# The attention's last product made transposed in three fp32r parts, and turned back through DRAM

## The reference

```python
    x = L0_attn_x
    x = x + _layernorm(_L0_attn_ref(_layernorm(x, axis=-1), L0_attn_gamma, L0_attn_beta, L0_attn_w_qkv, L0_attn_w_out, L0_attn_b_out), axis=-1)
    x = x + _layernorm(_L0_ffn_ref(_layernorm(x, axis=-1), L0_ffn_Wg, L0_ffn_Wu, L0_ffn_Wd), axis=-1)
    return x
```

```python
        qkv = jnp.einsum('bnc,ck->bnk', xn, w_qkv)
...
        k = jax.nn.softmax(k, axis=1)
        context = jnp.einsum('bnhd,bnhe->bhde', k, v)
        out = jnp.einsum('bhde,bnhd->bnhe', context, q)
        out = out.reshape(b, n, HEADS * DIM_HEAD)
        out = jnp.einsum('bnk,kc->bnc', out, w_out) + b_out
        return out + x
```

## Time and profile before

| what | value |
|---|---|
| median of the runs | 547.89 us |
| profiled execution, device time | 547.71 us |
| span of its trace | 545.9 us |
| PE busy | 538.5 us (99%) |
| DVE busy | 439.1 us (80%) |
| ACT busy | 344.5 us (63%) |
| POOL busy | 163.6 us (30%) |
| steady batch (100.00 to 165.43 us) | PE busy all the time at full granted clock |

### The profile page before, as it was taken

The page is one execution under the profiler, slowest core; times in us unless marked ns, Lnnn a source line. Parts: engine busy times, 40 slices in busy tenths (PEclk is TensorE's granted clock), DMA queues, the critical chain, the costliest instruction groups (busy, mean ns, idle before and its releaser), DMA issues.

```text
span 545.9 us, 8677 instructions
## 1 busy us (share of the span) xinstructions
PE 538.5 (99%) x2627; PEld 465.3 (85%) x2628; DVE 439.1 (80%) x975; ACT 344.5 (63%) x624; POOL 163.6 (30%) x211
## 2 busy tenths in 40 slices
PE   8999999999999999999999999999999999999996
PEld 5688888888888888888888888888888888888885
DVE  6796986999778987798878898689976888778666
ACT  5886867556675566755657566665667555655554
POOL 5797670336003450033501244022620033001001
PEclk9999999999999999999999999999999999999999
DMA  6354120210111110101202101021010200010000
GB/s 197 96 157 131 45 58 1 77 59 20 40 38 40 58 40 20 64 19 54 58 1 77 39 23 58 1 77 44 15 40 0 78 20 20 19 40 0 21 0 20
DMA packets 29614, 25.52 MB, mean 47 GB/s; under 512 B 3200, under 2 KB 22272, under 8 KB 29568
## 3 DMA queue, kind: packets, MB, share of 16 engines
q1 hardware_dynamic: 28272, 24.26, 14.2%
q10 hardware_dynamic: 1296, 0.72, 0.5%
HBM read 15.80 MB, written 9.18 MB: 46 GB/s over the span
## 4 chain that ended last, share of the span: by engine, by line
PE 96%; DVE 1%; DMA 1%; SPq 1%; ACT 0%; POOL 0%; issue 0%; POOLq 0%; DVEq 0%
PE acc_att_ps L1125 10%; PE acc_att_ps L1128 10%; PE acc_att_ps L1126 10%; PE gate_ps L1125 10%; PE up_ps L1125 10%; PE up_ps L1126 10%; PE gate_ps L1126 10%; PE up_ps L1128 10%; PE gate_ps L1128 10%; PE acc_att_ps L1183 1%; PE acc_att_ps L1171 1%; DMA w_raw<-in_L_ffn_Wu_dram 1%; PE acc_att_ps L1159 0%; PE acc_att_ps L1179 0%; DVE xh L1096 0%
## 5 line engine op out<-in xcount | busy, mean ns | idle before, releaser
L682 ACT ACTIVATE gs<-gate_ps 128x512 f32<-128x512 f32 x255 | 152.1, 597 | 177.8 <-PE gate_ps L1128 174.7
L922 DVE TENSOR_TENSOR h<-gs,up_ps 128x512 f32<-128x512 f32 x231 | 157.8, 683 | 86.6 <-PE up_ps L1128 84.2
L909 DVE TENSOR_TENSOR h_lo<-h,h_hi 128x512 fp32r<-128x512 f32 x231 | 172.8, 748 | 0.1
L659 ACT ACTIVATE h_hi<-h 128x512 fp32r<-128x512 f32 x231 | 143.9, 623 | 7.6 <-DVE h L922 7.1
L1125 PE MATMUL gate_ps<-x1nT_hi,wg_hi 128*128 128x512 f32 (+1 forms) x254 | 98.5, 388 | 0.0
L1125 PE MATMUL acc_att_ps<-h_hi,wd_hi 128*128 128x512 f32 (+1 forms) x256 | 96.8, 378 | 0.0
L1126 PE MATMUL acc_att_ps<-h_hi,wd_lo 128*128 128x512 f32 (+1 forms) x256 | 96.8, 378 | 0.0
L1128 PE MATMUL acc_att_ps<-h_lo,wd_hi 128*128 128x512 f32 (+1 forms) x256 | 96.8, 378 | 0.0
L1125 PE MATMUL up_ps<-x1nT_hi,wu_hi 128*128 128x512 f32 (+1 forms) x254 | 96.1, 378 | 0.0
L1126 PE MATMUL up_ps<-x1nT_hi,wu_lo 128*128 128x512 f32 (+1 forms) x254 | 96.1, 378 | 0.0
L1128 PE MATMUL up_ps<-x1nT_lo,wu_hi 128*128 128x512 f32 (+1 forms) x254 | 96.1, 378 | 0.0
(11 more groups left out here) (231 smaller groups left out, 531.9 us busy)
## 6 DMA issues: line engine op xcount, KB each, us to landing
w_raw<-in_L_ffn_Wg_dram SPq DMA_DIRECT2D x8, 256.0 KB, 3.1
w_raw<-in_L_ffn_Wu_dram SPq DMA_DIRECT2D x8, 256.0 KB, 3.0
w_raw<-in_L_ffn_Wd_dram SPq DMA_DIRECT2D x8, 256.0 KB, 3.1
x_in<-in_L_attn_x_dram SPq DMA_DIRECT2D x7, 256.0 KB, 2.8
t_dram_x1n<-t_blk_x1n SPq DMA_DIRECT2D x7, 256.0 KB, 2.0
t_out_x1n<-t_dram_x1n SPq DMA_DIRECT2D x28, 64.0 KB, 2.0
t_dram_acc<-t_blk_acc SPq DMA_DIRECT2D x7, 256.0 KB, 2.3
t_out_acc<-t_dram_acc SPq DMA_DIRECT2D x28, 64.0 KB, 2.0
```

Source lines behind the costliest of these rows:

```text
L659: act.activation(h_hi[s % NH][:, :], h_of(t, s)[:, :], ACT.Copy).then_inc(s_hhi, 1)
L682: act.activation(gs[q][:, :], gate_ps[q][:, :], ACT.Silu).then_inc(s_silu, 1)
L909: dve.tensor_tensor(h_lo[s % NH][:, :], h_of(t, s)[:, :], h_hi[s % NH][:, :].bitcast(F32), ALU.subtract).then_inc(s_hlo, 1)
L922: dve.tensor_tensor(h_of(t, s)[:, :], gs[q][:, :], up_ps[q][:, :], ALU.mult).then_inc(s_h, 1)
```

## The change

The attention's last product is made the other way round for batches 2 to 7 (b = 1 to 6 in `body`, c = 2 to 7). Instead of four fp32 products of 128 columns it is one group of three fp32r products with 512 moving columns, with G as the stationary operand (`G_hi`, `G_lo`) and the already split `xnT_hi`, `xnT_lo` as the moving one. The result has channels on the partitions. Batch 1 keeps the old form, and batch 0 is made apart from both.

Since z is wanted with tokens on the partitions, the result is turned: VectorE transposes the blocks (`z_T`, into the tile of E), SP stores and loads them, the loads going into `zn`. VectorE's `z` then adds `yb` to what was loaded. ScalarE writes `G_hi` in place of `G_sb`, and VectorE makes `G_lo` at the front of step 14. The places of the later stages move.

```diff
-DVE_AT = {"kmax": 2, "acc": 2, "E_T": 3, "next_stats": 6, "A": 10, "fin_stats": 10, "M": 12, "fin_scale": 12, "next_T": 14,
-          "z": 15, "z_stats": 15, "x1_stats": 20, "next_xnT_lo": 22, "x1n_T": 23, "x1n_lo": 29}
-ACT_AT = {"exp": 2, "G": 14, "next_xnT": 20, "next_xnT_hi": 21, "x1n_hi": 28}
+DVE_AT = {"kmax": 2, "acc": 2, "E_T": 3, "next_stats": 6, "A": 10, "fin_stats": 10, "M": 12, "fin_scale": 12, "G": 14,
+          "z_T": 15, "next_T": 16, "z": 18, "z_stats": 18, "x1_stats": 22, "next_xnT_lo": 23, "x1n_T": 25, "x1n_lo": 30}
+ACT_AT = {"exp": 2, "G": 14, "next_xnT": 21, "next_xnT_hi": 22, "x1n_hi": 29}
...
+        t_blk["z"] = t_blk["E"]
+        t_out["z"] = zn[:, :, :].rearrange("p j d -> p (j d)")
...
+                if not first and not last:
+                    store_blocks("z", s_z_blk, b)
                 if nxt:
                     store_blocks("x", s_xh_blk, b + 1)
+                if not first and not last:
+
+                    sp.wait_ge(s_x1, b)
+                    load_blocks("z", b)
+                if nxt:
                     load_blocks("x", b + 1)
...
+                if at == "G":
+                    dve.wait_ge(s_G, c)
+                    dve.tensor_tensor(G_lo[:, :], att_ps[:, 0:D], G_hi[:, :].bitcast(F32),
+                                      ALU.subtract).then_inc(s_G_lo, 1)
+                if at == "z_T":
+                    dve.wait_ge(s_attn_ps, c)
+                    dve.wait_ge(s_t_store["E"], c * 16)
+                    dve.transpose(grouped(t_blk["z"][:, :]), by_group(att_ps[:, :])).then_inc(s_z_blk, 1)
...
+                    else:
+                        dve.wait_ge(s_t_load["z"], (c - 1) * 64)
+                        dve.tensor_tensor(z[:, :, :].rearrange("p j (i r) -> p j i r", r=32), from_group(t_out["z"][:, :]),
+                                          yb[:, :, :].rearrange("p j (i r) -> p j i r", r=32), ALU.add).then_inc(s_z, 1)
...
+                    if c > 2:
+
+                        dve.wait_ge(s_t_store["z"], (c - 2) * 16)
...
+                if at == "attn" and not first:
+
+                    pe.wait_ge(s_G, c)
+                    pe.wait_ge(s_G_lo, c - 1)
+                    products(att_ps[:, :], G_hi[:, :], G_lo[:, :], xnT_hi[:, :], xnT_lo[:, :], True, True, s_xnT_lo,
+                             c - 1).then_inc(s_attn_ps, 1)
```

More of the change, by code:

```diff
@@ L27 @@
 MIDDLE = ("acc",)
-FRONT = ("xnT", "kmax", "E", "A", "M", "G", "z", "x1n_hi", "x1n_lo")
+FRONT = ("xnT", "kmax", "E", "A", "M", "G", "z_T", "z", "x1n_hi", "x1n_lo")
 FIRST_PE = {"A": 11, "M": 13, "G": 15, "attn": 16}
@@ L34 @@
 PE_AT = {"kT": 1, "A": 9, "M": 11, "G": 13, "attn": 14}
[L35 to L38 removed]
+DVE_AT = {"kmax": 2, "acc": 2, "E_T": 3, "next_stats": 6, "A": 10, "fin_stats": 10, "M": 12, "fin_scale": 12, "G": 14,
+          "z_T": 15, "next_T": 16, "z": 18, "z_stats": 18, "x1_stats": 22, "next_xnT_lo": 23, "x1n_T": 25, "x1n_lo": 30}
+ACT_AT = {"exp": 2, "G": 14, "next_xnT": 21, "next_xnT_hi": 22, "x1n_hi": 29}
+POOL_AT = {"yb": 4, "next_rstd": 7, "next_xn": 10, "fin_rstd": 11, "fin_out": 13, "z_rstd": 19, "x1": 19, "x1_rstd": 22}
 BUSY = {"start": 7, "w": 1, "U": 3, "z": 2, "xn": 2, "attn": 1, "x1n": 2}
@@ L139, in build @@
         G_sb = sb("G_sb", [P, D])
+        G_hi = sb("G_hi", [P, D], F32R)
+        G_lo = sb("G_lo", [P, D], F32R)
         z = sb("z", [P, J, D])
@@ L159, in build @@
         t_out = {k: sb(f"t_out_{k}", [P, N]) for k in turned}
-        t_dram = {k: nc.dram_tensor(f"t_dram_{k}", [P, N], F32) for k in turned}
+        t_blk["z"] = t_blk["E"]
+        t_out["z"] = zn[:, :, :].rearrange("p j d -> p (j d)")
+        t_dram = {k: nc.dram_tensor(f"t_dram_{k}", [P, N], F32) for k in (*turned, "z")}
         fn = sb("fn", [P, J, D])
@@ L267, in build @@
         s_G = sem("s_G")
+        s_G_lo = sem("s_G_lo")
         s_attn_ps = sem("s_attn_ps")
@@ L337, in build @@
         s_E_blk = sem("s_E_blk")
+        s_z_blk = sem("s_z_blk")
         s_x1n_blk = sem("s_x1n_blk")
-        s_t_store = {k: sem(f"s_t_store_{k}") for k in turned}
-        s_t_load = {k: sem(f"s_t_load_{k}") for k in turned}
+        s_t_store = {k: sem(f"s_t_store_{k}") for k in (*turned, "z")}
+        s_t_load = {k: sem(f"s_t_load_{k}") for k in (*turned, "z")}
         s_fn = sem("s_fn")
@@ L638, in attention @@
                     act.wait_ge(s_G_ps, c)
-                    act.activation(G_sb[:, :], att_ps[:, 0:D], ACT.Copy).then_inc(s_G, 1)
+                    act.activation(G_sb[:, :] if first else G_hi[:, :], att_ps[:, 0:D], ACT.Copy).then_inc(s_G, 1)
                 if at == "x1n_hi":
@@ L837, in attention @@
                                              in1=R_sb[:, :], op0=ALU.mult, op1=ALU.add).then_inc(s_M, 1)
+                if at == "G":
[6 more added lines that the diff above has]
+                    dve.transpose(grouped(t_blk["z"][:, :]), by_group(att_ps[:, :])).then_inc(s_z_blk, 1)
                 if at == "z":
                     dve.wait_ge(s_yb, c)
-                    dve.wait_ge(s_attn_ps, c)
-                    dve.tensor_tensor(z[:, :, :], att_v, yb[:, :, :], ALU.add).then_inc(s_z, 1)
+                    if first:
+                        dve.wait_ge(s_attn_ps, c)
+                        dve.tensor_tensor(z[:, :, :], att_v, yb[:, :, :], ALU.add).then_inc(s_z, 1)
+                    else:
+                        dve.wait_ge(s_t_load["z"], (c - 1) * 64)
+                        dve.tensor_tensor(z[:, :, :].rearrange("p j (i r) -> p j i r", r=32), from_group(t_out["z"][:, :]),
+                                          yb[:, :, :].rearrange("p j (i r) -> p j i r", r=32), ALU.add).then_inc(s_z, 1)
                 if at == "z_stats":
@@ L1179, in attention @@
                     pe.matmul(att_ps[:, 0:D], wqT[:, :], M_sb[:, :], start=True, stop=True).then_inc(s_G_ps, 1)
-                if at == "attn":
+                if at == "attn" and not first:
[3 more added lines that the diff above has]
+                             c - 1).then_inc(s_attn_ps, 1)
+                elif at == "attn":
                     pe.wait_ge(s_G, c)
```

## The result

The changed kernel takes 553.62 us (median of 4 runs, 553.42 to 554.15) against 547.97 us for the kernel before on the same chip: ratio 1.0100, 95% interval 1.0088 to 1.0112. It is slower by 5.65 us; 549.5 was predicted, with a range up to 552.3. The direction and the place were right, the size was not. The span of the profiled execution is 551.6 us, 5.7 more than before.

The account below looks back on a forecast made before the run. TensorE, busy 99% of the span, was taken to bound the kernel. Five waits of 0.55 us lose 2.75, six gains of 0.155 give 0.93: +1.8 us on 547.71, so 549.5 us, range 547.2 to 552.3.

Parts of the forecast that it names:

- the steps of the chain: z's way through DRAM in a steady batch: `next_T` ends, x's store issues, z loads issue and land, VectorE starts z at 124.45.
- The kT group: Three products with the same moving tiles into the same bank, 0.71 us, taken as the time of the new product.
- the start after a wait: TensorE's weight load follows VectorE's end by 0.06 us, its matmul at the earliest in the same 0.05 us.
- The gain of 0.185 us without a wait: At the attention's last product: 0.895 us for four fp32 products against 0.71 for three fp32r, 0.185 us a batch.
- the 0.155 us to be gained in each batch: Net gain at the attention's last product: 0.185 us less 0.03 for TensorE's wait on `G_lo`.
- The `h_lo` of 17: VectorE's operand for TensorE's down, done at 126.4 and wanted at 126.7: in time by 0.2 us only.
- the rivals (552.2): Loads at 2.5 us beside x's store, or `h_lo` of 17 late: 0.9 to 1.2 us a batch, 552.2 us; chance 0.18.
- These stages: Chain behind z's statistics up to `x1nT_lo`, at about 147.4, needed by the next batch's first gate at 149.3; costed at nothing.
- the rival that VectorE alone feels the wait: VectorE's pause at z is swallowed by three steps of lag: 547.0 us, or 546.7 with `G_lo` hidden; chance 0.12.
- the bound and the rival: z loads landing after 2.3 us make TensorE's wait 0.85 us; at 2.5 us, the 552.2 us case, chance 0.18.
- The Trainium skill's figure that I set aside: Each z load takes 2.15 us: TensorE's wait grows by 0.15 us and the sum by 0.75 us.

## Why the prediction was right and wrong

**Right.** TensorE's queue bounds the kernel; the loads of z stand behind x's store; VectorE waits 2.5 us (2.64 measured) in b = 1 to 5 and not in b = 6; TensorE stops ahead of the third product of the down in step 21; `G_lo` holds up the product by 0.02 to 0.15 us (0.05). Taking off the 0.22 us by which the trace starts later, the steps of the chain came close: `next_T` at 120.06 (119.96 predicted), the first z load at 121.23 (121.07), z at 124.72 (124.45). The stop itself is 0.61 us against 0.55 predicted.

**Wrong, by term.**

1. *The gap behind a stop*, which no step had: the product after one that waited comes 0.30 to 0.32 us later instead of 0.216 to 0.236. The kT group, my model for the new product, had not waited and so didn't show it; the earlier trace rows, which I used for the start after a wait, end with the product itself. The gain of 0.185 us without a wait was right, 0.19 with `G_lo` early. With a wait for `G_lo` of 0.05 instead of 0.03 it leaves 0.07 of the 0.155 us to be gained in each batch (0.5 us less in six), and makes each stop 0.10 longer. With the stop itself 0.06 us longer than predicted, b = 1 to 4 cost 0.68 each instead of 0.55: 0.5 us.
2. *The `h_lo` of 17, "in time, the latter by 0.2 us only"*, costed at nothing. The margin was read rightly. What failed is that I took the landing of a load as one number, 2.0 to 2.1 us. In b = 5 the fetch made it 3.3, the margin went and the step cost 2.03 instead of 0.55: 1.5 us. The case stood among the rivals (552.2), as a matter for all batches or none.
3. *"These stages have 1 us; I cost them at nothing."* The 1 us is what was left for x1n's loads, and the fetch took it in b = 1: 1.1 us. The experiment with z a step later shows that without TensorE's own delay it would have been more, 1.4 us.

0.5 + 0.5 + 1.5 + 1.1 = 3.6 us on the predicted 549.5 gives 553.1; with the 0.2 at the start it is 553.3, against 553.62.

The rows to see 2 and 3 by were there. Against the rival that VectorE alone feels the wait, the prediction says of the terms that "all repeat within 0.1 us from batch to batch". In its own trace the store of x lands after 2.0 to 2.1 us in b = 0 to 4 and after 2.9 in b = 5, beside a code packet, in the very batch that later had two places (view of DMA of the kernel before, 378 to 379 us):

```profile
q8 instruction: 1, 0.02, 5.9%
t_dram_x<-t_blk_x SPq DMA_DIRECT2D x1, 256.0 KB, 2.9
```

The earlier trace rows has a longest landing of 2.6 us, and the trace has other stores and loads through DRAM of 3.1 and 3.2 us. I used the median for the sum, and 2.3 and 2.5 us for the bound and the rival. A chain with 0.2 us to spare in one place and 1 us in another, passed five times, met the slow case in both places in each of the three traces of the changed kernel. With these two terms, 1.5 and 1.1 us, the forecast of 549.5 would have been 552.1; this is said afterwards, with their sizes known.

The Trainium skill's figure that I set aside ("DMA: Bandwidth & Descriptors", "Anatomy of one DMA", an estimate of 2.15 us for 64 KB) should not have been put beside these loads: the page gives that fit for DMAs issued from GpSimd, and these are issued by SP. The 24 z loads have a median of 2.0 us and go from 1.8 to 3.3.

## What to carry to other kernels

The chain through DRAM cost nothing here once its loads were issued as soon as its store had landed; look at what stands ahead of them in the DMA queue, and at what stands behind the waiting instruction on the engine that reads them. Where a chain that is passed many times has less than about 1.5 us to spare (the latest landing in the changed kernel, 3.5, less the median of 2.0), count on a late landing in one or two of the passes, and look in the trace of before for transfers that are late already. An operand that came 0.05 us too late for TensorE cost 0.12 (1.25 against 1.13 us around the product): make it a step earlier.

## What the runs showed of the hardware

- Program code comes in over the DMA engines of the data. In the changed kernel a packet of 16 KB of queue q8 comes every 23 to 32 us, and over all traces each keeps one engine busy for 0.9 to 1.8 us. They are TensorE's code: with 30 products more at TensorE's start they come 5 to 6 us earlier (22.1 to 16.7 us, 42.5 to 36.4), while those of the other code queue, q14, come 1 us later with the rest of that execution (14.9 to 16.0, 30.2 to 31.4). Of the 140 loads and stores through DRAM that were under way together with a q8 packet, 63 took over 2.7 us and up to 4.3, and of the 1625 beside none of either queue the longest took 2.6. The Trainium skill ("Runtime: NRT & Kernel Launch", "Instruction fetch mechanics") gives blocks of 16 KiB, which the q8 packets agree with (those of q14 have 8 KB), and calls the cost of crossing into the next one "mostly hidden". For the engine that runs the code no row here speaks against that; the transfers beside the packets are what the trace shows late.
- A matmul of 512 columns that waited for a semaphore is followed by a gap of 0.08 to 0.10 us. So is the first one behind the attention's products of 128 columns, without a wait (0.299 us to the next, 115.36 to 115.66 in the kernel before). Products of 512 columns right behind each other have none.
- Products whose moving tile is `xnT_hi` or `xnT_lo` come 0.23 to 0.24 us apart, those of the feed-forward 0.216, at the same clock and size.
- After stops of TensorE of 3.2 us (b = 2 to 4) and 4.5 us (b = 5) the granted clock was 0.50, the level of 1.2 GHz, over 3.4 or 6.8 us; after one of 3.2 us in b = 1 it stayed at 1.00.
